# First attention of a fused two-layer block: one more head of lead for key sides, corrections and loads, four buffers for bands and key sides, and another order in SyncE's steps

## The reference, cut to what matters

```python
Q, K, V = _heads(x @ Wq.T + bq), _heads(x @ Wk.T + bk), _heads(x @ Wv.T + bv)
rel_pos = jnp.clip(rel + 64, 0, 127)        # rel = key position - query position
p2c_pos = jnp.clip(-rel + 64, 0, 127)
scores = jnp.einsum('bhqd,bhkd->bhqk', Q, K) * scale
c2p = take_along_axis(einsum('bhqd,shd->bhqs', Q, pos_key) * scale, rel_pos)
p2c = swapaxes(take_along_axis(einsum('bhkd,shd->bhks', K, pos_query) * scale, p2c_pos))
scores = scores + c2p + p2c
ctx = softmax(scores) @ V
```

## Time and profile before

| what | value |
| --- | --- |
| median of 3 runs | 2092.57 us (2091.52, 2092.57, 2100.56) |
| the profiled execution's own time | 2092.16 us |
| its span | 2090.0 us |
| busy over the whole span | TensorE 83%, VectorE 69%, ScalarE 71% |
| mean granted TensorE clock | 0.937 |
| DMA queues, share of 16 engines' span | 66.1%, 403.66 MB |

### The profile page before, as it was taken

The page is one execution under the profiler, slowest core; times in us unless marked ns, Lnnn a source line. Parts: engine busy times, 40 slices in busy tenths (PEclk is TensorE's granted clock), DMA queues, the critical chain, the costliest instruction groups (busy, mean ns, idle before and its releaser), DMA issues. The chain is left out here.

```text
span 2090.0 us, 44501 instructions
## 1 busy us (share of the span) xinstructions
PE 1741.7 (83%) x11694; PEld 1049.1 (50%) x11694; DVE 1447.2 (69%) x3484; ACT 1476.3 (71%) x2600; POOL 79.7 (4%) x102
## 2 busy tenths in 40 slices
PE   5359999889898988874760899999999994999998
PEld 3135555555555555543540555656655652545544
DVE  5348888878888888854982888889888882324422
ACT  4338888888888888863871899999999992223222
POOL 0000000000000000001530000000000000000000
PEclk8659999999999999996985899999999997999999
DMA  6758888888888888846787777777777763100100
GB/s 192 240 169 258 253 255 253 261 245 253 257 258 255 254 245 253 255 124 170 249 300 232 199 215 213 211 211 213 214 211 214 211 164 101 35 20 25 35 5 10
DMA packets 432880, 404.38 MB, mean 193 GB/s; under 512 B 38522, under 2 KB 354098, under 8 KB 432690
## 3 DMA queue, kind: packets, MB, share of 16 engines
q1 hardware_dynamic: 432817, 403.66, 66.1%
HBM read 227.09 MB, written 175.77 MB: 193 GB/s over the span
## 5 line engine op out<-in xcount | busy, mean ns | idle before, releaser
L891 ACT ACTIVATE a_prob<-bank,a_negmax 128x512 f32<-128x512 f32 x1024 | 733.5, 716 | 81.6 <-DVE a_negmax L828 79.7
L828 DVE TENSOR_REDUCE a_negmax<-bank 128x1 f32<-128x512 f32 x1024 | 699.1, 683 | 0.1
L711 PE MATMUL bank<-a_ident,a_prob 128*128 128x128 f32 x4096 | 645.1, 280 | 53.2 <-ACT a_probt L898 43.9
L898 ACT COPY a_probt<-bank 128x512 f32<-128x512 f32 x1024 | 615.7, 602 | 82.4 <-PE bank L711 69.0
L711 PEld LDWEIGHTS bank<-a_ident,a_prob 128*128 128x128 f32 x4096 | 449.9, 141 | 172.9 <-ACT a_probt L898 69.1
L820 DVE TENSOR_TENSOR bank<-bank,a_band 128x128 f32<-128x128 f32 (+3 forms) x1024 | 350.5, 342 | 123.4 <-PE bank L692 68.9
L690 PE MATMUL bank<-a_stks 74*128 74x192 bf16 (+7 forms) x1024 | 324.4, 317 | 10.0 <-ACT a_prob L891 9.8
L724 PE MATMUL bank<-a_probt,a_vs 128*32 128x512 f32 x2048 | 273.9, 609 | 15.0 <-ACT a_probt L898 15.0
L690 PEld LDWEIGHTS bank<-a_stks 74*128 74x128 bf16 (+1 forms) x1024 | 100.3, 98 | 233.2 <-ACT a_prob L891 204.6
L808 DVE COPY_PREDICATED bank<-a_mask,bank 128x128 f32<-128x128 uint32 (+1 forms) x512 | 139.3, 272 | 90.7 <-PE bank L696 90.6
L692 PE MATMUL bank<-a_stks 74*128 74x320 bf16 (+5 forms) x768 | 200.9, 262 | 0.0
(11 more groups left out here) (176 smaller groups left out, 1568.9 us busy)
## 6 DMA issues: line engine op xcount, KB each, us to landing
a_band<-shear_b SPq DMA_DIRECT2D x128, 512.0 KB, 4.3
shear_a<-a_keyside SPq DMA_DIRECT2D x128, 256.0 KB, 3.3
a_sheared<-shear_a SPq DMA_DIRECT2D x128, 256.0 KB, 3.9
shear_b<-a_corr SPq DMA_DIRECT2D x128, 256.0 KB, 4.7
shear_e<-a_corr SPq DMA_DIRECT2D x128, 256.0 KB, 2.3
a_band<-shear_e SPq DMA_DIRECT2D x128, 256.0 KB, 3.3
a_stks<-stack SPq DMA_DIRECT2D x256, 96.0 KB, 2.5
a_stks<-stack SPq DMA_DIRECT2D x384, 48.0 KB, 2.6
```

The lines of the kernel that those rows point to most:

```text
L711: last = pe.transpose(turned_bank[k][:, n * 128:(n + 1) * 128], prob[h.slot % 2][:, n, k * 128:(k + 1) * 128], ident[:, :])
L828: v.tensor_reduce(negmax[h.slot % 2][:, n:n + 1], score[:, :], AX.X, ALU.max, negate=True).then_inc(maxed, 1)
L891: nc.scalar.activation(prob[h.slot % 2][:, n, :], score[:, :], ACT.Exp, bias=negmax[h.slot % 2][:, n:n + 1]).then_inc(exped, 1)
L898: nc.scalar.copy(probt[h.slot][:, k, :], turned_bank[k][:, :]).then_inc(copied, 1)
```

## The change

In the first attention the correction of head n+5 (was n+4), the key side of head n+7 (was n+6) and the stacks of head n+8 (was n+7) are made in step n. `band` and `keyside` get four buffers each, and the semaphores of the two DRAM writes become four each, one for each place. SyncE's list for a step is in another order, and the prologue of the phase too. The opening phase loads the stacks of 8 heads instead of 7. The second attention is unchanged in substance: its constants only lose their index.

```diff
-CORR_AHEAD, KEY_AHEAD, LOAD_AHEAD = {0: 4, 1: 5}, 6, {0: 7, 1: 8}
+CORR_AHEAD, KEY_AHEAD, LOAD_AHEAD = 5, 7, 8
...
                             if b > 3:
                                 first_head(2 * (b - 4))
-                                if b < B - 1:
-                                    first_head(2 * (b - 4) + 1)
+                                first_head(2 * (b - 4) + 1)
...
-                wide, bands = (WIN, 2) if rel else (REL, 4)
+                wide, bands = WIN if rel else REL, 4
...
-                    keyside = [sb(f"keyside{i}", [128, T]) for i in range(2)]
+                    keyside = [sb(f"keyside{i}", [128, T]) for i in range(4)]
...
-                    b_written = s("b_written")
+                    b_written = [s(f"b_written{i}") for i in range(4)]
...
+                    a_written = [s(f"a_written{i}") for i in range(4)]
...
                 def shear_a_read(sp, h):
-                    hold(sp, a_written, 16 * (h.n + 1))
+                    hold(sp, a_written[h.slot % 4], 16 * (h.use(4) + 1))
...
                 def shear_b_read(sp, h):
-                    hold(sp, b_written, 16 * (h.n + 1))
+                    hold(sp, b_written[h.slot % 4], 16 * (h.use(4) + 1))
...
                     if rel:
-                        if left > corr_ahead:
-                            shear_a_write(sp, Head(i, j + corr_ahead + 1))
-                        if left > 1:
+                        if left >= CORR_AHEAD + 1:
+                            shear_a_write(sp, Head(i, j + CORR_AHEAD + 1))
+                        if left >= CORR_AHEAD - 1:
                             hold(sp, added, 4 * (n + 1))
-                            shear_b_read(sp, Head(i, j + 2))
-                        if left > 2:
-                            shear_b_write(sp, Head(i, j + 3))
-                        if left > load_ahead - 1:
-                            hold(sp, maxed, 4 * n)
-                            head_load(sp, Head(i, j + load_ahead))
-                        if j % GROUP == 1 and left >= 10:
-                            tab_load(sp, Head(i, j + 7))
-                        if j % GROUP == GROUP - 1 and left >= 8:
+                            shear_b_write(sp, Head(i, j + CORR_AHEAD - 1))
+                        if left >= CORR_AHEAD + 1:
+                            shear_a_read(sp, Head(i, j + CORR_AHEAD + 1))
+                        if left >= CORR_AHEAD - 2:
+                            shear_b_read(sp, Head(i, j + CORR_AHEAD - 2))
+                        if left >= LOAD_AHEAD:
                             hold(sp, maxed, 4 * (n + 1))
-                            offset_load(sp, Head(i, j + 5))
-                        if left > corr_ahead:
-                            shear_a_read(sp, Head(i, j + corr_ahead + 1))
+                            head_load(sp, Head(i, j + LOAD_AHEAD))
+                        if j % GROUP == 0 and left >= LOAD_AHEAD + GROUP - 1:
+                            tab_load(sp, Head(i, j + LOAD_AHEAD))
+                        if j % GROUP == GROUP - 1 and left >= LOAD_AHEAD:
+                            offset_load(sp, Head(i, j + LOAD_AHEAD + 1 - GROUP))
...
                     def corr_out(act, h):
                         act.wait_ge(corr_mm, BASE + h.n + 1)
-                        act.wait_ge(b_written, BASE + 16 * (h.n - 1))
+                        old = h.before(2)
+                        act.wait_ge(b_written[old.slot % 4], BASE + 16 * (old.use(4) + 1))
```

More of the change, by code:

```diff
@@ L472, in attention_phase @@
                 if rel:
-                    key_mm, key_copied, a_written = (s(n) for n in ("key_mm", "key_copied", "a_written"))
+                    key_mm, key_copied = s("key_mm"), s("key_copied")
+                    a_written = [s(f"a_written{i}") for i in range(4)]
                     sheared_in = [s(f"sheared_in{i}") for i in range(4)]
@@ L483, in __init__, with before @@
                         self.n = unroll * i + at
+                    def before(self, heads):
+                        return Head(self.i, self.slot - heads)
                     def use(self, ring):
@@ new lines, in sync_step @@
+                        if j % GROUP == 0 and left >= LOAD_AHEAD + GROUP - 1:
+                            tab_load(sp, Head(i, j + LOAD_AHEAD))
+                        if j % GROUP == GROUP - 1 and left >= LOAD_AHEAD:
+                            offset_load(sp, Head(i, j + LOAD_AHEAD + 1 - GROUP))
+                    else:
+                        if left >= CORR_AHEAD:
+                            edge_write(sp, Head(i, j + CORR_AHEAD))
+                        if left >= CORR_AHEAD - 1:
+                            hold(sp, added, 4 * (n + CORR_AHEAD - bands))
+                            edge_read(sp, Head(i, j + CORR_AHEAD - 1))
+                        if left >= LOAD_AHEAD:
+                            if not isinstance(i, int) or n + LOAD_AHEAD >= unroll:
+                                hold(sp, maxed, 4 * (n + LOAD_AHEAD - unroll + 1))
+                            head_load(sp, Head(i, j + LOAD_AHEAD))
@@ L627, in _ @@
                         if rel:
-                            for j in range(load_ahead):
+                            for j in range(LOAD_AHEAD):
                                 sp.sem_inc(stk_in[j], per_stk)
@@ L762, in tensor_step @@
                                 weigh(pe, Head(i, j - j % GROUP - GROUP), j % GROUP)
-                            if not rel and k == 1 and left >= corr_ahead:
-                                edge(pe, Head(i, j + corr_ahead))
+                            if not rel and k == 1 and left >= CORR_AHEAD:
+                                edge(pe, Head(i, j + CORR_AHEAD))
                             if rel and k == 1 and left >= KEY_AHEAD:
@@ L767, in tensor_step @@
                                 key_side(pe, Head(i, j + KEY_AHEAD))
-                        if rel and left >= corr_ahead:
+                        if rel and left >= CORR_AHEAD:
                             pe.wait_ge(copied, BASE + 4 * own.n + 3)
-                            correction(pe, Head(i, j + corr_ahead))
+                            correction(pe, Head(i, j + CORR_AHEAD))
                     @block.tensor
@@ L776, in _ @@
                         if not rel:
-                            for j in range(corr_ahead):
+                            for j in range(CORR_AHEAD):
                                 edge(pe, Head(0, j))
@@ L783, in _ @@
                                 key_side(pe, Head(0, j))
-                                if j >= 2:
-                                    pe.wait_ge(corr_copied, BASE + j - 2)
-                                    correction(pe, Head(0, j - 2))
+                                if j >= 3:
+                                    pe.wait_ge(corr_copied, BASE + j - 3)
+                                    correction(pe, Head(0, j - 3))
+                            pe.wait_ge(corr_copied, BASE + CORR_AHEAD - 1)
+                            correction(pe, Head(0, CORR_AHEAD - 1))
                             pe.wait_ge(key_copied, BASE + KEY_AHEAD)
@@ L836, in key_out @@
                         v.wait_ge(key_mm, BASE + h.n + 1)
-                        v.wait_ge(a_written, BASE + 16 * (h.n - 1))
-                        v.tensor_copy(keyside[h.slot % 2][:, :], key_bank[:, :]).then_inc(key_copied, 1)
+                        v.wait_ge(a_written[h.slot % 4], BASE + 16 * h.use(4))
+                        v.tensor_copy(keyside[h.slot % 4][:, :], key_bank[:, :]).then_inc(key_copied, 1)
                     @block.vector
@@ L871, in vector_step @@
                                     finish(v, *ahead(i, j, k, score_ahead))
-                                if not rel and k == 3 and left >= corr_ahead:
-                                    edge_out(v, Head(i, j + corr_ahead))
+                                if not rel and k == 3 and left >= CORR_AHEAD:
+                                    edge_out(v, Head(i, j + CORR_AHEAD))
                                 if rel and k == 1 and left >= KEY_AHEAD:
@@ L926, in scalar_step @@
                                     group_out(act, Head(i, j - j % GROUP - GROUP))
-                            if rel and left >= corr_ahead:
-                                corr_out(act, Head(i, j + corr_ahead))
+                            if rel and left >= CORR_AHEAD:
+                                corr_out(act, Head(i, j + CORR_AHEAD))
                         for j in range(FIRST):
```

58 lines of the change are left out of this document (28 added, 30 removed).

## The result

The changed kernel took **2107.72 us**, the median of 8 runs (2105.58 to 2111.76), beside 2095.83 us for the kernel before, in 8 runs as well (2091.52 to 2100.56). The ratio is 1.0058, 95% interval 1.0045 to 1.0072: 11.9 us slower. Forecast were 2128 us and 36 us more. The profiled execution was the slowest of its runs, 2111.76 us with a span of 2109.7, so the two profiles stand 19.7 us apart and not 11.9. The changed kernel's lines are 3 to 13 higher than before: L832 is the band addition (L820 before), L741 the key side on TensorE, L551 the key side's write, L563 the correction's write, L557 the skewed read, L569 the band's read, L526 and L527 the stacks, L538 the tables.

What follows compares the result with a forecast made beforehand. No engine was full; late bands held up VectorE. SyncE's slower pace +38.3, prologue -4.5, opening +1.8 and semaphores +0.2 made +35.8 on 2092.16, so 2128 us; 8 in 10 range 2062 to 2166.

Steps and rivals of the forecast that it cites:

- late bands: First attention's steady stretch: VectorE waits for band reads, costing 30.6 us over 112 heads, which the longer lead removes.
- the sum for four late steps: SyncE, first attention: issue gaps, landing waits and occasional DMAs total 26.24 us, 6.56 us a head, +38.3 us.
- The DMAs once in four heads: SyncE's list: DMAs that come once in four heads cost 3.0 us plus 0.5 for the tables, together 3.5.
- the gaps: SyncE's late step: gaps of four DMA issues, 2.46 us a step, 9.84 us for four heads.
- W: SyncE's wait from issue of the key side's write to issue of the skewed read: 3.4 us, 2.7 after the store.
- the forecast alone: Case of the key side's round trip wait between 3.1 and 3.6 us: 2106 to 2148 us, chance 0.44.
- Prologue: Start of first attention, first key side to first score: -4.5 us, bounds 0 and -8.
- Opening and semaphores: Opening phase loads one more head's stacks, +1.8 us; five more semaphores in starting and clearing, +0.2 us.
- The short round trip: Rival: key side's write lands in 2.6 us every step, SyncE keeps pace, 2059 us; faster has chance 0.24.
- The full queue: Rival: key side's write takes 3.8 us to land, 6.86 us a head, 2162 us; chance 0.2.

Runs made afterwards that it cites:

- Loads first: Changed kernel with stack, table and offset loads right behind the key side's write, then correction's write, band's read, skewed read: 2056.88 us, ratio 0.9829 to before.
- half a band: Changed kernel with the band's read cut from 512 to 256 KB, leaving out part of the result: 2056.26 us, ratio 0.9823 to before.
- band's read first: Changed kernel with the band's read moved ahead of the correction's write, skewed read left in place: 2061.51 us, ratio 0.9879 to before.
- the new order alone: Kernel before, old leads, with the changed kernel's order of a step and the correction's write semaphore split in four: 2186.91 us, ratio 1.0464.
- the run with the read at the end: Changed kernel with the skewed read moved behind the stack, table and offset loads, ahead of the store: 2063.06 us, ratio 0.9873 to before.

## Why the prediction was right and where it was wrong

**Right: the bound before.** 5.945 us of compute a head and 30.6 us of late bands. Loads first, half a band and band's read first come out at 5.94 to 5.97 us a head.

**Right: what takes the gain back.** The band waits went, as forecast; the key side's round trip inside the step became SyncE's wait (2.2 to 174.7 us); TensorE's key side became the place where it showed, though behind the tables rather than the stacks, as a table load is the last DMA of its step; the loss came once in four heads. Taking the wait away (ratio 0.9873) and lengthening it (1.0553) move the time as the account says.

**Wrong: its size.** +38.3 us were forecast for 112 heads, +20.1 are in the profile. The step that failed is the sum for four late steps, 26.24 us. The round from 520.36 to 545.05 took 24.69. Term by term: the four waits were 2.08 + 3.67 + 3.14 + 3.23 = 12.1 us instead of 3 x 3.4 + 2.7 = 12.9, and it is the one after the store that was over-priced, 2.1 for 2.7, while 3.4 for the other three was right (mean 3.35). The DMAs once in four heads were 2.7 + 0.5 = 3.2 instead of 3.5. The rest, the gaps, were 9.4 instead of 9.84. Together 1.55 us too much, or 0.39 a head. It is no odd round: the eight from 395.48 to 595.40 us took 25.0 us on average, 6.25 a head, only 0.03 over the kernel before.

The other way something was missing, since the mean over all 112 heads is 6.398, or 25.6 us a round. The long rounds, up to 28.49 us, show two things that the sum didn't have. In seven of them the gap in the second step was 4.1 to 5.7 us and not 3.3 to 3.9; I don't know why. And the granted clock of TensorE fell behind some of the late heads. Two heads in a row in the view of windows (columns as in the earlier trace rows):

```profile
702.18:709.54 7.36, 5.65 (x45) 3.43 (x44) 5.14 (x15) 5.08 (x9) 0.00 (x0) 0.94 0.77 219
709.54:717.95 8.41, 8.22 (x47) 4.79 (x46) 5.13 (x15) 5.36 (x9) 0.00 (x0) 0.65 0.81 278
```

In the first of them TensorE stood for the tables until 707.58. From 709 to 715 us the granted clock was 0.50, the lower level of 1.2 GHz, and about the same number of matmuls kept TensorE busy for 8.22 us instead of 5.65. Nine such heads (mean clock 0.65 to 0.87), each right behind a late one, took 13.0 us more together than 5.945 us each; the kernel before has three (0.74 or 0.75), with 2.4 us. The 13.0 us give the size of this part only roughly and are not its share in the +20.1: SyncE catches up meanwhile, so the next loss can be smaller, and in some of the late heads themselves the clock was low as well. The prediction had no term for the clock. SyncE also waits for ScalarE's copy, 50.1 us in 710, where I had let it wait for nothing but W; most of that lies inside the gap from write to skewed read and adds little by itself.

The errors partly cancel; the size was right only within a factor of two in the profile, and three in the medians. The direction held partly by luck: at the pace of those eight rounds the stretch would have cost about 3 us (estimated, 112 x 0.03) and the kernel would have come out even. The forecast was also put on a profiled execution of the kernel before that lay 3.7 us under the median of its 8 runs. And the bounds of the forecast alone, 2106 and 2148, are some 3 us above what its own sum gives at W = 3.1 and 3.6.

**Wrong: how it was split.** The prediction named the wait that became bare, but not what makes it harmful. The early skewed read by itself made the kernel before 1.45% faster. It costs when the band's read and the loads both stand behind it; with the band's read in the wait (0.9879) or the loads in it (0.9870) it doesn't. With the new leads the total of SyncE's list still tells these apart, as one issue a step less in the open brings it under 4 x 5.945 us. With the old leads it doesn't: the new order alone cost 4.6%, where I had expected 1 to 3 from the total, and there the sum leaves out when in the step each transfer leaves.

**The small terms.** Prologue -4.5 forecast, -2.8 found: the last skewed read was again what the first score waited for. Opening and semaphores +2.0 forecast, +0.1 found: the two loads did take their 1.8 us on SyncE (96.97 to 98.76), but the first key side stood where it was. The first eight heads took 46.92 us instead of 45.00, which I hadn't priced. The 0.2 us for semaphores can't be told apart in any run.

**The rivals.** The short round trip needed W = 2.6 in every step; it was 3.1 to 3.7 in three of four, and 2.98 at least in any such step of the stretch. The full queue fell with the run with the read at the end, where the same bytes went through faster.

**What stays open.** The profile pair shows 19.7 us and the medians 11.9, because one profiled execution lay 4.0 us above its median and the other 3.7 below; the runs spread over 6 and 9 us. And no run holds TensorE's clock apart: in the stretch the granted clock was 0.97, 0.99 before and 1.00 in the fastest version, and the heads counted above give its part only roughly.

## What to carry to other kernels

In a hand-written DMA list, ask of each wait what stands behind it: a transfer that is due soonest goes ahead of a bare wait, and whatever is due late goes into it. Deeper buffers are worth something only while the issuing list keeps its pace; add its round once (issues, waits, and what comes every fourth step) and compare it with what the compute engines need. When a change has several parts, price each order and each depth by itself: here the leads alone gained 1.2%, the early skewed read alone 1.5%, and it was the band's read, moved behind both, that turned them into a loss. And where a forecast is the difference of two nearly equal sums, look at what an error of a few per cent does to it: 0.16 us in a head of 6.56 halved this one.

## What was not expected of the hardware

A 256 KB write and the wait for its landing took 2.1 us behind the store and the load of v (520.36 to 522.44), and 3.7 behind a band's read. With 256 KB less in that read, 3.7 became 2.7. The Trainium skill (DMA: Bandwidth & Descriptors, anatomy of one DMA) fits 2.0 us plus bytes over 436 GB/s for another issue path, which makes an estimate of 2.6 us for such a transfer. The 2.1 us measured here lie below that and the 3.7 above.

With the early skewed read alone, the longest wait of VectorE for a band fell from 2.1 us to 1.1, with the same bytes, leads and buffers, and a pace 4% higher. The band's read still left early in the step; whether SyncE's short stops keep the queue from filling ahead of it, no run tests.

A wait of a few us on TensorE can cost twice. Behind a head of 7.36 us, in which TensorE stood for the tables, the clock was at its lower level for some 6 us and the next head took 8.41; but after other late heads, such as that of 7.43 us, the next took 5.95.
